# An attention and mixture-of-experts layer on one core: four planned columns of heads, and float16 projections dealt out in half tiles

## The chip, the cores and the metric

The kernel runs on one core of a Trainium2 chip. A core has a matmul engine (TensorE; PE in the profile, with PEld for its weight loads), a vector engine (DVE), a scalar engine (ACT), a general engine (POOL) and a queue engine (SP) that issues most transfers. The metric is the device time of one execution in microseconds (us), the median of several.

## The reference

One transformer layer over 4096 tokens of width 256, in float32. Cut to what matters here:

```
q, k, v = lora(x, Wq, Aq, Bq), lora(x, Wk, ...), lora(x, Wv, ...)   # 16 heads of 16
s   = q @ k.T / 4 + slope[h] * (i - j);  s = -1e30 where j > i       # ALiBi, causal
x   = layernorm(x + (softmax(s) @ v) @ Wp.T)
probs = softmax(x @ Wg);  top 2 of 8 experts, capacity 1076 each
y   = sum over the two of gate * (gelu(x @ W1[e] + b1[e]) @ W2[e] + b2[e])
x   = layernorm(x + y)
```

## The kernel before

**Stages.** First a start-up: effective weights from the low-rank factors, projections of token blocks 0 and 1. Then one long loop over "turns" does attention; projections of blocks 2 to 7 and the routing of blocks 0 to 6 are woven into it. Then the last block is routed, the experts run, and a last layernorm ends.

**A turn.** Tokens come in 8 blocks of 512 queries (QB), keys in tiles of 128. A head needs only `TILES[h]` key tiles, since the bias kills distant ones: 2, 3, 4, 6, 8, 12, 16, 23 and then 32 eight times. Heads 2i and 2i+1 are a pair, which shares its rows of the operand tiles `kop` and `qop` (one at partition 0, one at 64). `plan()` deals pairs to two lanes; a unit is one key tile of one pair, and a turn has one unit of each lane. Its length in a lane is that of the longer head of the pair, and the shorter head leaves its place empty. On the diagonal a key tile needs only the queries from `q0` on, so a unit is 512, 384, 256 or 128 queries wide.

In turn t, PE makes the scores of the turn's two units into `ps_s` (L1024, float16), then `pv(t - LAG)`, LAG being 2: four probability-times-value products in float32 (L1040), one in each group of 32 columns of the array, all into the bank `ps_o`. ACT takes the exponential of each unit (L1097, one instruction for both heads). `ps_s` holds three units (SLOTS_S), so PE may score unit p once the exponential of unit p - 3 is done. POOL zeroes the masked corner of a diagonal unit (L1119). When a job (a pair over all its key tiles) has ended, DVE copies the lane's half of `ps_o` to `acc` (`evict`, L1149), SP stores it, and the first product of the lane's next job waits for the copy.

**Woven in**, all through the one bank `ps_r`, by tables from turn to work: `TILE_AT` (a projection tile, 128 outputs by 512 tokens, two float32 matmuls by `pe_half`, L439, one ahead of `pv` and one behind it, then `dve_head` and `dve_tail`), `VALUE_AT` (values of 128 tokens, L460), `NORM_AT` (norms for an overflow bound, L450), `ROUTE_AT` (output projection and router logits of 128 tokens, L1369) with `SCALE_AT` two turns ahead of it (DVE: shuffle, reciprocal, multiply, L1395 to L1399), `CHOOSE_AT`, `COUNT_AT` and `SCATTER_AT` (top two, places, indirect stores by POOL). Projection tiles stand 3 turns apart, value tiles 2, routing tiles 3. Projections of a block end long ahead of its first turn: the last stand at turn 197, and the loop has 430 turns.

**The flag.** DVE works out whether the float16 scheme is in range (L578 to L589). At `FLAG_TURN`, turn 202, every engine but POOL reads the flag and jumps over the general path (class `General`), which this data does not take. Routing starts behind it.

## Time and profile before

| | |
|---|---|
| median of 3 runs | 1354.06 us (1353.83 to 1354.3) |
| the profiled execution | 1366.05 us |
| its span, first to last instruction | 1363.6 us |
| busy over the span | PE 1208.5, ACT 919.7, DVE 604.4, POOL 352.9 us |
| first exponential of attention | at 41.5 us |
| last one | ends at 873.7 us |

"Busy" of an engine is the union of its instructions. A matmul's end is modelled, so the start-to-start distance says more than its length. Next to each group stands how long its engine was idle just before it and who released it. PEclk is the granted clock of TensorE, 1.00 for 2.4 GHz and 0.50 for 1.2 GHz.

### The profile page before, as it was taken

What the parts mean: (1) busy time and instruction counts of PE and PEld (TensorE: products, weight loads), DVE (VectorE), ACT (ScalarE), POOL (GpSimd) and SP (SyncE); (2) the same over time, 40 slices, a digit from 0 to 9 for tenths busy, and PEclk for the clock granted to TensorE, in tenths of its full rate; (3) what the DMA queues carried; (4) which work ended last, traced back from release to release, by engine and by line L of the source; (5) the groups of instructions that cost most, each with busy time, mean ns of one, the idle gap of its engine ahead of it and who ended that gap; (6) DMA issues with size and microseconds to landing.
All of it is one profiled execution on the core that took longest, in us unless ns stands there. A gap on an engine that the chain in (4) does not pass through costs nothing. (4 is left out here: it accounts for less than half of the span.)

```text
span 1363.6 us, 23733 instructions
## 1 busy us (share of the span) xinstructions
PE 1208.5 (89%) x8566; PEld 500.0 (37%) x8566; DVE 604.4 (44%) x1635; ACT 919.7 (67%) x1200; POOL 352.9 (26%) x374
## 2 busy tenths in 40 slices
PE   7799999999998999999899989625999998999990
PEld 3222222222222212222212211113877876877780
DVE  4232222212122265555446430073676676676756
ACT  2588888888987998899889999514354354344314
POOL 2321211100010013222330330023435534534430
PEclk9899999999999999999998998956999999999995
DMA  6952323213122021402211100154235333322216
GB/s 150 174 104 70 89 84 82 75 62 72 38 67 49 20 63 57 105 31 75 64 58 50 35 33 5 42 175 149 44 103 120 41 100 104 59 72 26 30 20 246
DMA packets 81187, 103.71 MB, mean 76 GB/s; under 512 B 12394, under 2 KB 66389, under 8 KB 81073
## 3 DMA queue, kind: packets, MB, share of 16 engines
q1 hardware_dynamic: 63952, 77.23, 20.7%
q0 software_dynamic: 15744, 23.83, 8.3%
q10 hardware_dynamic: 1376, 1.18, 0.5%
q8 instruction: 65, 1.06, 0.3%
q14 instruction: 50, 0.40, 0.1%
HBM read 56.76 MB, written 48.01 MB: 77 GB/s over the span
## 5 line engine op out<-in xcount | busy, mean ns | idle before, releaser
L1097 ACT ACTIVATE prob<-ps_s 128x1024 f32<-128x1024 f32 (+3 forms) x859 | 721.9, 984 | 118.0 <-PE ps_s L1024 111.8
L1040 PE MATMUL ps_o<-prob,v_aug 128*17 128x512 f32 (+3 forms) x3294 | 443.5, 575 | 17.2 <-DVE acc L1149 6.2
L1024 PE MATMUL ps_s<-qop,kop 51*128 51x512 f16 (+3 forms) x1647 | 280.5, 373 | 33.1 <-ACT prob L1097 10.5
L1024 PEld LDWEIGHTS ps_s<-qop,kop 51*128 51x128 f16 x1647 | 67.5, 93 | 407.0 <-ACT prob L1097 334.8
L1792 PE MATMUL ps_y<-w2s,hs 128*128 128x256 bf16 (+1 forms) x1728 | 199.5, 273 | 0.6 <-DVE yb L1869 0.6
L1776 PE MATMUL ps_h<-xs,w1s 128*128 128x384 bf16 (+1 forms) x1152 | 182.9, 318 | 7.8 <-ACT hid L1839 7.0
L1839 ACT ACTIVATE hid<-ps_h,b 128x384 f32<-128x384 f32 (+1 forms) x192 | 105.1, 560 | 123.0 <-PE ps_h L1776 95.1
L1119 POOL TENSOR_SCALAR_AFFINE_SELECT prob<-prob 128x256 f32<-128x256 f32 (+1 forms) x172 | 67.9, 402 | 436.7 <-ACT prob L1097 434.7
L1792 PEld LDWEIGHTS ps_y<-w2s,hs 128*128 128x128 bf16 (+1 forms) x1728 | 167.4, 99 | 18.2 <-DVE yb L1869 0.7
L1733 POOL DMA_INDIRECT result<-y,entry x72 | 112.0, 1555 | 179.6 <-DVE y L1874 149.2
L1149 DVE COPY acc<-ps_o 64x512 f32<-64x512 f32 x64 | 44.1, 689 | 232.4 <-PE ps_o L1040 223.6
L1776 PEld LDWEIGHTS ps_h<-xs,w1s 128*128 128x128 bf16 x1152 | 111.8, 99 | 73.2 <-ACT hid L1839 10.5
L1040 PEld LDWEIGHTS ps_o<-prob,v_aug 128*17 128x17 f32 x3294 | 58.3, 95 | 162.4 <-issue 105.3
L1885 DVE TENSOR_TENSOR hs<-hid,hs 128x384 bf16<-128x384 f32 (+1 forms) x192 | 105.9, 552 | 6.6
L1883 DVE CAST hs<-hid 128x384 bf16<-128x384 f32 (+1 forms) x192 | 87.9, 458 | 43.3 <-ACT hid L1839 42.4
L1830 ACT ACTIVATE xs<-ps_x 128x512 bf16<-128x512 bf16 (+1 forms) x72 | 40.1, 570 | 93.1 <-PE ps_x L1764 93.1
L1522 POOL DMA_INDIRECT slots_x<-xsplit,dest_all x64 | 63.8, 996 | 106.7 <-DVE xsplit L1500 65.1
L1633 POOL TENSOR_TENSOR w1s<-w,w1s 128x2048 bf16<-128x2048 f32 x8 | 32.5, 4067 | 107.8 <-ACT w1s L1627 92.5
L1869 DVE TENSOR_TENSOR yb<-ps_y,b 128x256 f32<-128x256 f32 (+1 forms) x72 | 30.3, 421 | 60.6 <-PE ps_y L1792 58.4
L1397 DVE RECIPROCAL den<-den 128x256 f32<-128x256 f32 x32 | 56.1, 1753 | 1.1
L439 PE MATMUL ps_r<-x_all 128*128 128x512 f32 x96 | 54.0, 644 | 0.0
L1874 DVE TENSOR_SCALAR y<-yb,weight 128x256 f32<-128x256 f32 (+1 forms) x72 | 45.9, 638 | 13.4 <-DMA result<-y,entry 8.4
(148 smaller groups left out, 651.0 us busy)
## 6 DMA issues: line engine op xcount, KB each, us to landing
w<-in_W SPq DMA_DIRECT2D x16, 1024.0 KB, 7.6
slots_x<-empty POOLq DMA_DIRECT2D x12, 520.0 KB, 4.0
qop<-fparts_q SPq DMA_DIRECT2D x42, 128.0 KB, 4.5
xe<-slots_x SPq DMA_DIRECT2D x8, 650.0 KB
x_all<-in_xT SPq DMA_DIRECT2D x8, 512.0 KB, 5.7
fparts_k<-x_all SPq DMA_DIRECT2D x16, 256.0 KB, 2.2
fparts_q<-x_all SPq DMA_DIRECT2D x16, 256.0 KB, 2.4
attnT<-acc SPq DMA_DIRECT2D x128, 32.0 KB
```

The costliest lines, as they stand in the source:

```text
L1024: mm = pe.matmul(ps_s[:, u.p % SLOTS_S, e, u.q0:], o.key(e, u.i, u.kt), o.query(e, u.i, u.b, u.q0), start=True, stop=True)
L1040: mm = pe.matmul(ps_o[c:c + VW, u.q0:], o.v[:, u.kt, 2 * u.i + e], prob[:, t % RING, n, e, u.q0:], start=u.first, stop=end)
L1097: act.activation(prob[:, t % RING, n, u.heads[0]:2, u.q0:], ps_s[:, u.p % SLOTS_S, u.heads[0]:2, u.q0:], ACT.Exp, scale=1.0 / (SCALE * SCA ...
L1119: pool.affine_select(own, own, [[0, len(u.heads)], [1, P]], ALU.is_ge, 0.0, base=0, channel_multiplier=-1).then_inc(masked, 1)
L1397: dve.reciprocal(r.den[:, s % 2], r.den[:, s % 2]).then_inc(r.inverted, 1)
L1522: pool.indirect_dma_start(out=r.slots_x, out_offset=bass.IndirectOffsetOnAxis(ap=r.dest_all[:, n, m:m + 1], axis=0), in_=r.xsplit[:, m // ...
L1733: pool.indirect_dma_start(out=result, out_offset=bass.IndirectOffsetOnAxis(ap=entry[0:n, u, k:k + 1], axis=0), in_=y[0:n, k % 3], in_offse ...
L1776: mm = pe.matmul(ps_h[:, q % 4, 0:w], w1s[:, u, i1, c, m * P:(m + 1) * P], xs[:, u, i2, c, a:a + w], start=(t == 0 and c == 0), stop=(t == ...
L1792: mm = pe.matmul(ps_y[0:n, (ST * u + k) % 2, 0:D], hs[:, (3 * u + sbk) % 2, i1, m, o:o + n], w2s[:, u, i2, m, :], start=(t == 0 and m == 0 ...
L1839: act.activation(hid[:, q % 4, 0:w], ps_h[:, q % 4, 0:w], ACT.Gelu_apprx_tanh, bias=b1[:, e, q % HC:q % HC + 1]).then_inc(gelu, 1)
L1883: dve.tensor_copy(hs[:, sl, 0, q % HC, 0:w], hid[:, q % 4, 0:w]).then_inc(h_high, 1)
L1885: dve.tensor_tensor(hs[:, sl, 1, q % HC, 0:w], hid[:, q % 4, 0:w], hs[:, sl, 0, q % HC, 0:w], ALU.subtract).then_inc(h_low, 1)
```

## The change

**A plan of four columns.** `columns()` now plans each of the four array columns (two in each lane, one for the heads at partition 0 and one for those at 64) for itself. A column starts its next head as soon as its last has ended, so the two heads of a unit may belong to different pairs and even blocks. Four heads of full length are ordered so that their four diagonal tiles fall in the same turns. Heads 6 and 7 swap their halves of the rows, for which the key and query parts of tiles 0 and 2 are stored with three transfers instead of one, and the bias rows with two more. The loop has 417 turns instead of 430; turns in which the tiles are not all equally wide number 20 instead of 69. Exponentials number 854 (859 before) for the same 780,800 columns; where the two tiles of a unit differ in width, each has its own. Over the turns, the widest tile sums to 199,552 columns (211,328 before). A column that ends is copied alone or with its neighbour: 116 copies (64 before) and 256 stores (192 before).

**Projections in float16 halves.** x and the weights are split into a high and a low float16 part on DVE (`dve_split_x` in four turns for each of six blocks, `dve_split_weights` in four turns once; the last two of each four are maxima for the bound). A half tile is 128 by 256 and takes six float16 matmuls (three part products, two chunks); DVE empties it at once (`dve_half`).

**One piece a turn, spread over 340 turns.** `projections()` spaces the 82 projection pieces evenly up to their due turns; routing pieces take free turns, at least 2 from the next piece. A piece now stands between scores and `pv` of its turn, after a wait that the piece before has left `ps_r`. Routing of block 0 starts at turn 160 (its loads at 150) instead of 214; within a block most routing tiles have a piece 2 turns ahead of them. The set-up of the router stands in turn 76.

**The branch** moves to turn 376, behind the routing, and POOL takes it too. Its general path repeats the routing and is longer. Bias rows of blocks 2 to 7 are loaded with their keys and no longer ahead of the loop. x1 of the routing is kept for two blocks instead of eight.

```
-    for _k in range(4):
-        TILE_AT[_t + 3 * _k] = (_n, _k)
+        due += [(FIRST_TURN[n] - 9, ("half", n, k, h)) for k in range(4) for h in range(2)]
+        due += [(FIRST_TURN[n] - 7, ("norm", n))]
+        due += [(DIAG_TURN[n] - 3, ("value", n, s)) for s in range(KT)]
...
+        z = min(range(i, len(due)), key=lambda z: ((due[z][0] - begin) / (z + 1 - i), -z))
+        for k in range(i, z + 1):
+            at[begin + (due[z][0] - begin) * (k - i) // (z + 1 - i)] = due[k][1]
...
+        for i, (a, b) in enumerate(FPARTS):
+            for c in range(2):
+                mm = pe.matmul(out, j.ws[:, a, m // 2, c, (m % 2) * P:(m % 2 + 1) * P], j.xs[:, b, c, cols],
+                               start=(i == 0 and c == 0), stop=(i == len(FPARTS) - 1 and c == 1))
...
+            dve.tensor_copy(j.xs[:, 0], x).then_inc(j.xs_high, 1)
...
+            dve.tensor_tensor(j.xs[:, 1], x, j.xs[:, 0], ALU.subtract).then_inc(j.xs_done, 1)
...
+                    row = HALF * job.lane + 32 * job.heads[0][0]
+                    rows = slice(row, row + 32 * len(job.heads))
+                    dve.tensor_copy(acc[rows, a], ps_o[rows]).then_inc(evicted[job.lane], 1)
...
-                    if t in TILE_AT:
-                        j.pe_half(pe, *TILE_AT[t], 0, ps_r[:])
+                    if t in PIECE_AT:
+                        bank_free(*BEFORE.get(t, ("norm", 1)))
+                        piece(*PIECE_AT[t])
                     if t >= LAG:
                         pv(t - LAG)
-                    if t in TILE_AT:
-                        j.pe_half(pe, *TILE_AT[t], 1, ps_r[:])
```

On PE, in the projections of block 4, before: `ps_r<-x_all` is half a float32 projection tile, `ps_s` scores, `ps_o` value products.

```order
L1024 MATMUL ps_s<-qop,kop 128x512 x4
L439 MATMUL ps_r<-x_all 128x512
L1040 MATMUL ps_o<-prob,v_aug 17x512 x4
L439 MATMUL ps_r<-x_all 128x512
L1024 MATMUL ps_s<-qop,kop 128x512 x2
L1024 MATMUL ps_s<-qop,kop 128x384 x2
L1040 MATMUL ps_o<-prob,v_aug 17x512 x4
L1024 MATMUL ps_s<-qop,kop 128x384 x2
L1024 MATMUL ps_s<-qop,kop 128x256 x2
L1040 MATMUL ps_o<-prob,v_aug 17x512 x4
```

And after, near the same place: `ps_r<-xs_half,ws_half` is a half tile.

```order
L1234 MATMUL ps_s<-qop,kop 128x512 x4
L1250 MATMUL ps_o<-prob,v_aug 17x512 x4
L1234 MATMUL ps_s<-qop,kop 128x384 x4
L564 MATMUL ps_r<-xs_half,ws_half 128x256 x6
L1250 MATMUL ps_o<-prob,v_aug 17x512 x4
L1234 MATMUL ps_s<-qop,kop 128x256 x4
L1250 MATMUL ps_o<-prob,v_aug 17x512 x4
L1234 MATMUL ps_s<-qop,kop 128x128 x4
L1250 MATMUL ps_o<-prob,v_aug 17x384 x4
```

What moved: a tile's two pieces around one `pv` became one piece ahead of it, and the diagonal widths 384, 256 and 128 stand in all four columns at once instead of in one lane beside a full-width one.

On DVE, in the routing of a block, before: `den` and `aT` are the scale, `slogit` and `x_all` the tile's results, `acc` an eviction of both lanes.

```order
L1397 RECIPROCAL den<-den 128x256
L1399 TENSOR_TENSOR aT<-aT,den 128x2x128
L1403 TENSOR_TENSOR slogit<-ps_r,xg 128x8
L1404 TENSOR_TENSOR x_all<-ps_r,x_all 128x256
L1149 COPY acc<-ps_o 64x512 x2
```

After, in the routing of block 1:

```order
L1641 RECIPROCAL den<-den 128x256
L1643 TENSOR_TENSOR aT<-aT,den 128x2x128
L1390 COPY acc<-ps_o 32x512 x2
L696 TENSOR_SCALAR x_all<-ps_r,less 128x256
L707 SCALAR_TENSOR_TENSOR x_all<-ps_r,less,x_all 128x256
L711 TENSOR_TENSOR sq<-x_all 128x256
L1390 COPY acc<-ps_o 32x512
L1639 STREAM_SHUFFLE den<-total 128x256
```

What moved: between the scales of the routing now stand the halves of block 6 and evictions of single columns.

## Rows read from the trace of the kernel before

**Rows 1.** The page, two groups: count, busy, mean ns, idle before.

```profile
L1097 ACT ACTIVATE prob<-ps_s 128x1024 f32<-128x1024 f32 (+3 forms) x859 | 721.9, 984 | 118.0 <-PE ps_s L1024 111.8
L1040 PE MATMUL ps_o<-prob,v_aug 128*17 128x512 f32 (+3 forms) x3294 | 443.5, 575 | 17.2 <-DVE acc L1149 6.2
```

**Rows 2.** Busy time by stretch: start:end, us, engines (instructions), PEclk, DMA share, GB/s.

```profile
422.00:560.00 138.00, 127.55 (x863) 30.84 (x863) 59.27 (x194) 120.01 (x144) 24.35 (x33) 0.96 0.21 53
...
sum 832.20, PE 785.76 PEld 183.18 DVE 273.18 ACT 721.85 POOL 158.39; mean PE 98.22 PEld 22.90 DVE 34.15 ACT 90.23 POOL 19.80
```

**Rows 3.** Timeline of ACT, two projection tiles: start, us, count, [idle before].

```profile
319.30 5.61 ACT L1097 ACTIVATE prob<-ps_s 128x1024 f32<-128x1024 f32 x6 [1.21 <-PE ps_s L1024]
326.12 5.60 ACT L1097 ACTIVATE prob<-ps_s 128x1024 f32<-128x1024 f32 x6 [1.21 <-PE ps_s L1024]
```

**Rows 4.** Timeline of PE, same stretch: the second half of a tile, then scores.

```profile
317.75 1.13 PE L439 MATMUL ps_r<-x_all 128*128 128x512 f32 x2
...
318.81 0.61 PE L1024 MATMUL ps_s<-qop,kop 51*128 51x512 f16 x4
```

**Rows 5.** Timeline of PE through value tiles two turns apart.

```profile
153.49 1.05 PE L1040 MATMUL ps_o<-prob,v_aug 128*17 128x512 f32 x8 [0.36 <-DVE acc L1149]
...
155.56 0.61 PE L1024 MATMUL ps_s<-qop,kop 51*128 51x512 f16 x4
...
157.08 0.61 PE L1024 MATMUL ps_s<-qop,kop 51*128 51x512 f16 x4
157.62 1.05 PE L1040 MATMUL ps_o<-prob,v_aug 128*17 128x512 f32 x8
158.60 1.16 PE L460 MATMUL ps_r<-x_all 128*128 128x264 f32 x4
159.69 0.61 PE L1024 MATMUL ps_s<-qop,kop 51*128 51x512 f16 x4
```

**Rows 6.** Groups by line in the expert stage, 1250 to 1300 us.

```profile
L1792 PE MATMUL ps_y<-w2s,hs 128*128 128x256 bf16 (+1 forms) x228 | 26.5, 273 | 0.0
...
L1792 PEld LDWEIGHTS ps_y<-w2s,hs 128*128 128x128 bf16 (+1 forms) x229 | 22.1, 99 | 2.4
```

**Rows 7.** Timeline of DVE, PE and ACT in the routing of block 1.

```profile
521.88 1.75 DVE L1397 RECIPROCAL den<-den 128x256 f32<-128x256 f32 x1
...
524.53 0.69 DVE L1149 COPY acc<-ps_o 64x512 f32<-64x512 f32 x1
...
525.37 1.91 PE L1040 MATMUL ps_o<-prob,v_aug 128*17 128x512 f32 x8 [2.04 <-DVE acc L1149]
...
529.53 1.02 ACT L1097 ACTIVATE prob<-ps_s 128x1024 f32<-128x1024 f32 x1 [3.89 <-PE ps_s L1024]
```

**Rows 8.** Timeline at the branch, turn 202, and at the set-up behind it.

```profile
438.31 0.60 PE L1024 MATMUL ps_s<-qop,kop 51*128 51x512 f16 x4 [3.02 <-issue]
...
443.07 1.94 ACT L1097 ACTIVATE prob<-ps_s 128x1024 f32<-128x1024 f32 x2 [2.33 <-PE ps_s L1024]
```

**Rows 9.** Timeline of the start-up: DVE on 512 columns, SP and PE.

```profile
10.28 0.69 DVE L514 SCALAR_TENSOR_TENSOR prob<-prob 128x512 f32<-128x512 f16 x1
11.01 0.43 DVE L516 TENSOR_SCALAR prob<-prob 128x512 f16<-128x512 f32 x1
...
15.01 0.60 SPq L312 DMA_DIRECT2D kop<-bias  x2
...
19.60 1.38 SPq L402 DMA_DIRECT2D fparts_k<-x_all  x2
...
26.05 2.74 ACTq L318 DMA_DIRECT2D qop<-fparts_q  x6
...
40.83 1.36 PE L1024 MATMUL ps_s<-qop,kop 51*128 51x512 f16 x6 [5.58 <-DMA qop<-fparts_q]
```

**Rows 10.** One DVE instruction with two inputs: all eight, then the last.

```profile
L1447 DVE TENSOR_TENSOR gap<-top 128x4 f32<-128x4 f32 x8 | 11.2, 1402 | 0.3
...
910.11 0.17 DVE L1447 TENSOR_TENSOR gap<-top 128x4 f32<-128x4 f32 x1
```

More of the change, by code:

```diff
@@ L88 @@
 assert sorted(TILES) == TILES
[L92 to L108 removed]
+COLS = 4
@@ L120, in plan, with runs @@
         steps.append(step)
     return steps, jobs
-STEPS, JOBS = plan()
+def runs(tiles):
+    if len(tiles) == 2 and tiles[0].q0 == tiles[1].q0:
+        return [(0, 2)]
+    return [(e, e + 1) for e in tiles]
 LAG = 2
@@ L128 @@
 ACCS = 4
+STEPS, JOBS = plan()
+UNITS = [u for s in STEPS for u in s if u]
 N_STEPS = len(STEPS)
-LAST_P = {b: max(u.p for s in STEPS for u in s if u and u.b == b) for b in range(NB)}
+LAST_P = {b: max(u.p for u in UNITS if any(a.b == b for a in u.tiles.values())) for b in range(NB)}
+FREED = {}
+for _n in range(2):
+    for _e in range(2):
+        _ends = [j for j in JOBS if j.lane == _n and any(e == _e for e, _, _ in j.heads)]
+        for _t, _s in enumerate(STEPS):
+            if _s[_n] and _e in _s[_n].tiles and _s[_n].tiles[_e].first:
+                FREED[_t, _n, _e] = max([j.number + 1 for j in _ends if j.end < _t], default=0)
@@ L161 @@
[L161 to L177 removed]
+BLOCK_TURNS = {b: [t for t in range(N_STEPS) for u in STEPS[t] if u and any(a.b == b for a in u.tiles.values())] for b in range(NB)}
@@ L729, in sync @@
                                      y.acc[32 * h + DH:32 * h + VW]).then_inc(y.a_stored, 16)
+            y.attended(sp)
+            for n in range(NB - 1):
+                y.r.load(sp, n, 1)
+                y.r.store_base(sp, n)
             y.leave(sp)
@@ L960, in _ @@
                 j.load_queries(sp, 1)
-                for b in range(2, NB):
-                    o.load_bias(sp, j.bias, b)
                 r.load_constants(sp)
```

634 lines of the change are left out of this document (406 added, 228 removed).

## The prediction

> **What bounds the kernel now.** I read the page first, then the busy time by stretch, then the timelines of single turns. The page gives PE the most busy time, 1208.5 of 1363.6 us, but a matmul's modelled length overlaps its neighbours, so this decides nothing. What the diff touches is the attention loop, 832.2 us, in which ACT is busy for 721.85 [rows 2]: it waits for 110 us, nearly all of it for scores from PE (111.8 of the 118.0 us over the whole kernel) [rows 1]. The exponentials are the same columns before and after (780,800), in 5 instructions fewer. So the loop can't fall under some 722 us, and all that the change can win lies in those 110 us.
>
> Why ACT waits shows in the turns. Six full exponentials take 5.61 us [rows 3] and two take 1.94 [rows 8], so a turn of two costs (5.61 - 1.94) / 2 = 1.83 us. PE needs 1.52 for the same turn: scores start at 155.56 and again at 157.08 [rows 5]. So PE has 0.32 us a turn to spare. What is woven in must fit into it, but for what the three score slots buffer. Rows 3 show a projection tile every third turn: ACT's runs start 6.82 us apart instead of 5.61, 1.21 lost. The sum agrees: a half tile holds PE for 1.06 us (317.75 to 318.81) [rows 4], a tile for 2.1, against 3 x 0.32 = 0.96 to spare; the rest, 1.16, is about the 1.21 idle. A value tile holds PE for 1.09 us (158.60 to 159.69), and with two turns between them the distance is 4.13 us (155.56 to 159.69) [rows 5], 0.46 more than 2 x 1.83. So **the rate of PE's woven-in work over two to four turns** bounds the projection stretches.
>
> Behind 422 us another cause joins: DVE comes late. In rows 7 an eviction starts only at 524.53, since the scale of a routing tile (its reciprocal alone 1.75 us) and its results stood ahead of it. PE then waits 2.04 us, runs on at half clock (products in 1.91 us instead of 1.05), and ACT is idle for 3.89. By stretch PEclk falls to 0.96 there [rows 2]. In the plan of before three evictions stand one turn behind a scale.
>
> **The change part by part**, made against the profiled 1366.05 us (12.0 above the median).
>
> 1. *Projection tiles.* 24 tiles that cost ACT 1.21 us each go: 29.0 us. In their place come 48 halves of six matmuls. A 256-column 16-bit matmul runs at 26.5 / 228 = 0.116 us in the expert stage [rows 6], and a full-array piece costs 0.2 on top (a value tile: 4 x 264 columns at two cycles are 0.88, measured 1.09). So a half is 0.70 + 0.2 = 0.9 us. They stand 2 to 5 turns apart, typically 2.75 in blocks 2 and 3, which gives 0.88 to spare: about nothing is lost. Gain 29, between 22 (0.15 lost at each half) and 31.
>
> The rows show loads of such weights, 229 of 99 ns, beside the matmuls: both in one stretch of 50 us, the 256-column group with its loads covered. The Trainium skill ("TensorE: Matmul & The Clock Gate", Part 3) says that a weight load overlaps a running matmul only when its row group differs, and all rows are used here. The trace does not agree: the 228 matmuls with their loads end to end would need 49 us of PE, and they ran beside 152 others in 50. What uncovered loads would give is rival E.
>
> 2. *Value tiles.* 28 at 0.46 us, 12.9 in all. Their distance to the next piece grows to 2.4 to 4 turns, where 1.09 stands against 0.8 to 1.3. Left over: some 3. Gain 10, between 5 and 13.
>
> 3. *The plan.* ACT's work stays. On PE a product's time follows the widest tile: 11,776 columns fewer at 0.98 us for 512 (157.62 to 158.60 [rows 5]) are 22.5 us. That counts only where PE is late, in the turns around the diagonal next to pieces. I take half, 11; bounds 0 and 22.
>
> 4. *Routing tiles.* Same length and count (28), but from 3 turns apart, which just about fitted (1.09 against 0.96), to 2 behind another piece in most cases. If 17 of them find no slack, 17 x 0.43 = 7 us. Loss 6, bounds 0 and 12.
>
> 5. *Evictions.* 52 more. An eviction at a PE that runs ahead of ACT is free; at a late one it costs the 0.36 us of rows 5 (153.49). Bounds 0 and 19; I take 4, because part 1 gives PE its lead back.
>
> 6. *DVE.* The x and weight splits add 28 instructions on 1024 columns: by rows 9, twice 0.43 for each of 7 high parts and twice 0.69 for the 21 others: 35 us of DVE, which was idle two thirds of the loop. Its cover is the next turn's length; where a split, a scale and an eviction meet (turns 259 to 261) the cover is gone and the cost is a wait as in rows 7. Evictions one turn behind a scale number 4 instead of 3. Loss 5, bounds 0 and 15. POOL shares something with DVE: the same small two-input instruction takes 0.17 us alone and 1.40 on average with POOL at work [rows 10]. The Trainium skill ("SBUF — State Buffer", Who interferes with whom) has a rule for it: a DVE instruction with two inputs or in a two-port mode and one of POOL block each other. The row agrees. Nine of the 28 splits stand in diagonal turns, where POOL's masks gate PE: at 1.38 us each at most 12 us, inside the bound of 15.
>
> 7. *Moved at no cost.* The branch costs the same at turn 376 as at 202 (PE 3.02 us idle, then the set-up, ACT another 2.33 [rows 8]); the flag is long there. POOL takes it when its scatters are issued. The longer bias store (two more transfers and a landing) holds SP from 15.01 on; SP's next store is not ready before 19.60, which leaves 4.6 us. The first score waits for queries that ACT issues at 26.05 and that land near 40.8 [rows 9]; three transfers instead of one for two tiles move neither. Behind the loop, 490 us, nothing changes.
>
> Sum: -29 - 10 - 11 + 6 + 4 + 5 = **-35 us**. Profiled 1331; on the median, 1354.06 - 35 = **1319 us**.
>
> **Rivals.**
>
> *A. PE gets ahead and stays there.* All 22 us of the plan count, routing and evictions cost nothing, DVE 3: -29 - 10 - 22 + 3 = -58, and two of the waits as in rows 7 lose their half clock, another 4: -62, 1292. For it: the sum of widest tiles falls in just the turns where pieces stand. Against: routing tiles at 2 turns have no slack by rows 5.
>
> *B. PE stays the bound.* Every new eviction costs 0.36 (19 us), routing 12, the plan brings nothing, and a half loses 0.15: -22 - 10 + 19 + 12 = -1, 1353. Half-way between this and the forecast: -18, 1336. For it: the stretches up to 422 us run at PE's rate now.
>
> *C. DVE becomes the gate, slower.* 116 evictions and 28 splits share a queue with 28 scales, each a reciprocal of 1.75 us [rows 7] and two more instructions, and the halves' three instructions each, now in the same turns. Each meeting costs what rows 7 show, 3.9 us of ACT with the low clock. It takes (35 + 3) / 3.9 = 10 more meetings than in before to end slower; 14 would give 1374. Against: the plan's table has one more by the strict count, and DVE is busy 273 of 832 us.
>
> *D. It doesn't do what it says.* Waits on `ps_r` or for the split of x take the place of the shorter matmuls, within 2 us of 1354. Against: the high and low parts are made 5 and 4 turns ahead of the first half.
>
> *E. Uncovered weight loads.* Six loads of 0.099 us [rows 6] in each of 48 halves lie on PE: 28.5 us, of which little is covered; -35 + 25 = -10, 1344. Against it are rows 6 themselves, in which they are covered.
>
> **How the numbers follow.** Forecast (1305 to 1333) 0.50; A (under 1305) 0.17; B 0.17, of which 0.15 under 1351; E 0.02; D 0.04, of which 0.03 within 0.2%; C 0.10. The range takes in A's value and B to beyond its half-way: 1290 to 1345, with B's upper part, D and C left out, under 0.2. A measurement here can tell 0.2% (2.7 us) from no change. Faster: 0.50 + 0.17 + 0.15 + 0.02 + 0.01 = 0.85; same 0.02 + 0.03 = 0.05; slower 0.10.
>
> **What would show it.** Right: the loop takes some 797 us from first to last exponential with ACT's busy time still near 722; around a half, PE's next row starts 0.9 us later and ACT shows no idle time; value tiles show gaps under 0.2. Part 4 is right if ACT's remaining gaps stand in 422 to 700 us behind routing tiles. Wrong for part 1: halves of over 1.2 us or gaps of 0.5 behind them. Wrong for parts 5 and 6: waits of PE for evictions of over 25 us in all (6.2 now [rows 1]), or a PEclk under 0.95 in a stretch. Wrong for part 7: a first score after 43 us, or a tail of other than 490 us.

## The result: 0.7% faster, a quarter of what was forecast

The changed kernel takes 1345.12 us (median of 4 runs, 1343.81 to 1346.38), the kernel before on the same chip 1354.18 (1353.83 to 1354.59): ratio 0.9933, 95% interval 0.9916 to 0.995. That is 9 us less; 35 were forecast.

The runs were made in six groups, each on one chip, and the groups fell on two levels: in three of them the kernel before takes 1354 to 1356 us, in three 1364 to 1366. They are called the **1355 level** and the **1365 level** here, and ratios are to the kernel before in the same group. What makes the level isn't known. It doesn't change within a group, but the record has chip number 15 for a group of either level, so it isn't shown to be a property of the chip. The changed kernel gave 0.9933 and 0.9904 at the first level and **1.012** at the second: the same change is 9 to 13 us faster or 14 us slower. The profiled execution of before (1366.05 us) agrees with the second level, the profiled execution of after (1345.55) with the first, so the 20.5 us between the two profiles flatter the change. Single executions at a lower granted clock, 200 to 630 us longer than the others, occurred in a few groups, and the ratios leave them out.

**The page of after**, the groups that answer to rows 1, and the half tiles:

```profile
L1330 ACT ACTIVATE prob<-ps_s 128x1024 f32<-128x1024 f32 (+3 forms) x854 | 721.3, 980 | 101.9 <-PE ps_s L1234 100.5
L1250 PE MATMUL ps_o<-prob,v_aug 128*17 128x512 f32 (+3 forms) x3294 | 422.6, 575 | 29.0 <-DVE acc L1390 18.3
...
L564 PE MATMUL ps_r<-xs_half,ws_half 128*128 128x256 f16 x288 | 40.0, 275 | 9.1 <-DVE x_all L1648 4.3
```

ACT's work is what it was (721.3 us; 721.9 in rows 1), and its idle time fell only from 118.0 to 101.9. What PE waits for evictions rose from 6.2 to 18.3 us. The third line holds a wait of a kind that was nearly absent before: PE waits until DVE has emptied `ps_r`. By the groups of PE in the loop:

```profile
L564 PE MATMUL ps_r<-xs_half,ws_half 128*128 128x256 f16 x288 | 40.0, 275 | 9.1 <-DVE x_all L1648 4.3 <-DVE x_all L709 2.2 <-DVE xg L720 1.3
L580 PE MATMUL ps_r<-x_all 128*128 128x264 f32 x112 | 34.4, 432 | 1.6 <-DVE x_all L1648 1.6
L1613 PE MATMUL ps_r<-wp,aT 128*128 128x264 f32 x112 | 32.7, 415 | 8.6 <-DVE x_all L1648 4.9 <-DVE x_all L707 2.2 <-DVE xg L720 1.5
...
L1618 PE MATMUL ps_r<-counts,before 128*128 128x32 bf16 x7 | 1.3, 186 | 3.2 <-DVE xg L720 1.5 <-DVE x_all L709 0.9 <-DVE run L1708 0.7
```

With two small groups more these waits are 24.3 us (1.7 before). Together with the evictions PE waits 42.6 us for DVE where it waited 7.9, as the profile names its waits.

The names leave out a part. Some waits of the products are put down to ACT or to "issue" (9.1 us before, 8.8 after). But the exponentials of a product are two turns old by then, and each of these waits ends 0.10 or 0.15 us behind the end of an eviction, just as those put down to DVE do. Counted so, PE waits for evictions 15.4 us before and 27.1 after. An example from the version with both repairs (below), DVE and then PE:

```profile
146.24 0.68 DVE L1391 COPY acc<-ps_o 32x512 f32<-32x512 f32 x1
147.02 1.05 PE L1250 MATMUL ps_o<-prob,v_aug 128*17 128x512 f32 x8 [0.31 <-ACT prob L1330]
```

**By stretch**, as rows 2 (start:end, us, then busy time and instructions of PE, PEld, DVE, ACT and POOL, PEclk, DMA share, GB/s):

```profile
422.00:560.00 138.00, 123.38 (x909) 31.94 (x902) 78.68 (x228) 120.39 (x139) 29.57 (x39) 0.99 0.22 60
560.00:700.00 140.00, 127.24 (x916) 31.95 (x916) 69.32 (x231) 120.82 (x138) 28.29 (x36) 0.96 0.22 59
...
sum 815.43, PE 740.77 PEld 185.92 DVE 344.07 ACT 721.36 POOL 158.93; mean PE 123.46 PEld 30.99 DVE 57.35 ACT 120.23 POOL 26.49
```

The loop takes 815.4 us from first to last exponential (832.2 before, at the other level), with PE 45 us less busy and DVE 71 us more (344.07 against 273.18).

**Where the loop loses time.** I take each turn from the end of its last exponential back to that of the turn before, and subtract what its exponentials need back to back (0.917 us for 1,024 columns by rows 3 and 8: (5.61 - 1.94) / 4; 0.702, 0.488, 0.27 and 0.17 for 768, 512, 256 and 128 by the same traces). The excess is put down to the piece that stands in the turn before it:

| excess of ACT's turns, us | before | after | after, both repairs (below) |
|---|---|---|---|
| projection: 24 tiles, then 48 halves | 38.1 | 27.0 | 18.8 |
| 28 value tiles | 22.4 | 19.6 | 18.4 |
| routing tiles and counts | 28.5 | 29.9 | 20.8 |
| norms, set-up | 0.5 | 2.4 | 1.6 |
| turns behind no piece | 36.8 | 31.1 | 22.5 |
| sum | 126.4 | 110.0 | 82.1 |

The column of before is at the 1365 level and the two others at the 1355 level, so a part of the differences is the level's; it is sized below.

By block the changed kernel won 25 us in blocks 2 to 4 (52.5 before, 27.6 after), lost 5 in blocks 0 and 1, and lost 11 in block 6 (17.0, then 28.3).

**One place where it is lost.** PE, DVE and ACT in the projections of block 3, in the order of the engines:

```profile
155.02 0.61 PE L1234 MATMUL ps_s<-qop,kop 51*128 51x512 f16 x4
155.56 1.05 PE L1250 MATMUL ps_o<-prob,v_aug 128*17 128x512 f32 x8
156.55 0.61 PE L1234 MATMUL ps_s<-qop,kop 51*128 51x512 f16 x4
158.35 0.83 PE L564 MATMUL ps_r<-xs_half,ws_half 128*128 128x256 f16 x6 [1.19 <-DVE x_all L709]
```

```profile
156.68 0.70 DVE L1390 COPY acc<-ps_o 32x512 f32<-32x512 f32 x1 [3.12 <-PE ps_o L1250]
157.41 0.42 DVE L698 CAST x_all<-ps_r 128x256 f16<-128x256 f32 x1
157.87 0.42 DVE L709 TENSOR_TENSOR x_all<-ps_r,x_all 128x256 f16<-128x256 f32 x1
```

```profile
155.51 3.77 ACT L1330 ACTIVATE prob<-ps_s 128x1024 f32<-128x1024 f32 x4 [0.22 <-PE ps_s L1234]
160.58 2.85 ACT L1330 ACTIVATE prob<-ps_s 128x1024 f32<-128x1024 f32 x3 [1.29 <-PE ps_s L1234]
```

A half issued at 153.28 was done by 154.04. But DVE's queue holds an eviction ahead of emptying it, and that eviction waits for the products that PE starts at 155.56. So DVE is idle for 3.12 us with a full `ps_r`, empties it at 157.41, and the next half, which stands right behind the scores of its turn, waits 1.19 us and holds the products and the next scores behind it. ACT pays 1.29.

**The worst place**, turn 264, where an eviction of two columns, a maximum, a scale and the half that follows meet. DVE, then PE and ACT:

```profile
555.99 1.41 DVE L1390 COPY acc<-ps_o 32x512 f32<-32x512 f32 x2 [2.44 <-PE ps_o L1250]
557.43 1.22 DVE L681 TENSOR_REDUCE peak<-xs_half 128x1 f32<-128x1024 f16 x1
...
559.05 1.75 DVE L1641 RECIPROCAL den<-den 128x256 f32<-128x256 f32 x1
...
561.37 0.41 DVE L1648 TENSOR_TENSOR x_all<-ps_r,x_all 128x256 f32<-128x256 f32 x1
```

```profile
561.84 1.06 PE L564 MATMUL ps_r<-xs_half,ws_half 128*128 128x256 f16 x6 [2.70 <-DVE x_all L1648]
562.84 1.91 PE L1250 MATMUL ps_o<-prob,v_aug 128*17 128x512 f32 x8
```

```profile
565.39 2.86 ACT L1330 ACTIVATE prob<-ps_s 128x1024 f32<-128x1024 f32 x3 [4.42 <-PE ps_s L1234]
```

PE waits 2.70 us for `ps_r`, its products then run in 1.91 us instead of 1.05 (half clock, as in rows 7), and ACT is idle for 4.42 us. The two evictions in a row of 555.99 are of a kind too: where columns of both lanes end in one turn, the second lane's next product waits for both copies.

### The profile page after: what moved, and what is told of

Read it like the earlier page. It is cut to its first block and busy times, and to the rows that moved or that the text cites. A ratio compares the mean times of both kernels' runs of the same rounds, so it can differ in the third digit from the quotient of the medians.

```text
span 1343.8 us, 24544 instructions
## 1 busy us (share of the span) xinstructions
PE 1164.5 (87%) x8759; PEld 503.3 (37%) x8759; DVE 676.8 (50%) x1791; ACT 918.9 (68%) x1195; POOL 353.4 (26%) x382
## 5 line engine op out<-in xcount | busy, mean ns | idle before, releaser
L1330 ACT ACTIVATE prob<-ps_s 128x1024 f32<-128x1024 f32 (+3 forms) x854 | 721.3, 980 | 101.9 <-PE ps_s L1234 100.5
L1250 PE MATMUL ps_o<-prob,v_aug 128*17 128x512 f32 (+3 forms) x3294 | 422.6, 575 | 29.0 <-DVE acc L1390 18.3
L1234 PE MATMUL ps_s<-qop,kop 51*128 51x512 f16 (+3 forms) x1647 | 267.1, 372 | 26.8 <-ACT prob L1330 8.9
L1390 DVE COPY acc<-ps_o 32x512 f32<-32x512 f32 (+1 forms) x116 | 79.7, 687 | 307.7 <-PE ps_o L1250 300.1
L1234 PEld LDWEIGHTS ps_s<-qop,kop 51*128 51x128 f16 x1647 | 62.4, 94 | 404.9 <-ACT prob L1330 360.1
L2138 DVE CAST hs<-hid 128x384 bf16<-128x384 f32 (+1 forms) x192 | 91.6, 477 | 46.0 <-ACT hid L2094 44.9
L2140 DVE TENSOR_TENSOR hs<-hid,hs 128x384 bf16<-128x384 f32 (+1 forms) x192 | 102.1, 532 | 6.6
L2129 DVE TENSOR_SCALAR y<-yb,weight 128x256 f32<-128x256 f32 (+1 forms) x72 | 48.6, 675 | 12.5 <-DMA result<-y,entry 7.6
L564 PE MATMUL ps_r<-xs_half,ws_half 128*128 128x256 f16 x288 | 40.0, 275 | 9.1 <-DVE x_all L1648 4.3
```

Source lines behind the costliest of these rows:

```text
L1234: mm = pe.matmul(ps_s[:, u.p % SLOTS_S, e, a.q0:], o.key(e, a.h, a.kt), o.query(e, a.h, a.b, a.q0), start=True, stop=True)
L1250: mm = pe.matmul(ps_o[c:c + VW, a.q0:], o.v[:, a.kt, a.h], prob[:, t % RING, n, e, a.q0:], start=a.first, stop=a.last)
L1330: act.activation(prob[:, t % RING, n, e:z, q0:], ps_s[:, u.p % SLOTS_S, e:z, q0:], ACT.Exp, scale=1.0 / (SCALE * SCALE)).then_inc(exp_done, 1)
L1390: dve.tensor_copy(acc[rows, a], ps_o[rows]).then_inc(evicted[job.lane], 1)
L2138: dve.tensor_copy(hs[:, sl, 0, q % HC, 0:w], hid[:, q % 4, 0:w]).then_inc(h_high, 1)
L2140: dve.tensor_tensor(hs[:, sl, 1, q % HC, 0:w], hid[:, q % 4, 0:w], hs[:, sl, 0, q % HC, 0:w], ALU.subtract).then_inc(h_low, 1)
```

## The experiments

All ratios are to the kernel before in the same group of runs, with the 95% interval.

**The kernels themselves, in other groups.** Nothing is edited.

> The changed kernel itself, beside its variants on one chip. In the runs so far the variants showed stalls of ACT and DVE of 2 to 6 us in the turns of the scatters (both wait for updates from PE that come late), 12 to 19 us in all, and the changed kernel, on another chip, none. If these stalls belong to the chip or to the dense scatters in any of the new plans (theory S), they show here too, 10 us or more, and the ratio rises from 0.993 toward 1.000. If they come from what the variants changed (theory V), there are none, and the ratio is again 0.992 to 0.995.

1378.66 us where before has 1364.57: 1.012 (1.0089 to 1.0152). Up to turn 180 its turns exceed ACT's own time just as in the first profile (10.3, 6.9 and 10.4 us in blocks 2 to 4 in both). Then 23.3, 43.0 and 26.7 stand against 17.1, 28.3 and 14.4, and the new losses are at turns 190, 221, 255, 282, 310, 341 and 370 and next to them, one place in each of the seven blocks, in the eight turns in which POOL issues its scatters, as theory S has it.

> The changed kernel once more, as the measure for the three beside it on the same chip. It gave 0.9933 on one chip and 1.012 on another, where ACT waited 2 to 5 us for updates from PE that came late, each time behind five or more scatters that POOL had issued back to back (1.29 us apart). If that depends on the chip: either value, near 0.993 or near 1.01. If it is chance from run to run: something between, with a wide spread.

1342.91 us where before has 1355.7: 0.9904 (0.9886 to 0.9922), none of these losses. So it isn't chance from run to run: it goes with the level. The kernel before was also profiled once more, at the 1365 level: 1363.35 us, its excess some 125 us and spread over the kinds of piece as in the table. It had been expected near 1354 if the first profile held unusual waits, or near 1366 if profiling costs 12 us as such; neither holds, since executions of that group without a profile took 1365.88 too. There is no profile of it at the 1355 level.

**The piece behind the products on PE.**

```
+                    if t >= LAG:
+                        pv(t - LAG)
                     if t in PIECE_AT:
                         bank_free(*BEFORE.get(t, ("norm", 1)))
                         piece(*PIECE_AT[t])
-                    if t >= LAG:
-                        pv(t - LAG)
```

> The changed kernel with the piece back behind the products of its turn on PE (as a value tile stood in before); DVE's order as in the changed kernel. Theory Q: the wait for ps_r comes when DVE has long been released by these products, so waits for ps_r fall below 6 us as well, and the time is 1328 to 1337 us. Theory R: 1341 to 1347 us. If this gains and the other order on DVE doesn't (or the other way round), the cause is where the piece stands and not the wait.

At the 1365 level 1352.72 us, 0.9901 (0.987 to 0.9932), which is 0.022 under the changed kernel in another group of that level. The waits for `ps_r` fell from 24 to 7 us, those for evictions from 18 to 6. But the losses in the scatter turns were there. This edit alone was never run at the 1355 level. The next runs are about the scatters.

**Scatters spaced.** One every second turn, and with a wait for the exponentials of the turn before (two edits in one, never tried apart):

```
-        SCATTER_AT[_t + 2 + _k] = (_n, _k)
+        SCATTER_AT[_t + 2 + 2 * _k] = (_n, _k)
...
+                        pool.wait_ge(exp_done, max(u.exps for u in STEPS[t - 1] if u))
                         r.scatter(pool, *SCATTER_AT[t], r.scattered)
```

> The changed kernel with the scatters of a block in every second turn instead of every turn, each behind the exponentials of the turn before it, so that POOL issues them about 3.7 us apart and no longer in one run of 1.29 us apiece. Theory S (the dense run of scatters makes PE's updates late; the old plan had fewer such runs, since masks stood between its scatters): no wait of ACT over 2.2 us behind scatters, and on a chip like the second 15 to 25 us faster than the changed kernel, ratio 0.990 to 0.996; on a chip like the first within 3 us of it. Rival (the stalls come from the loads and stores that meet there, or from the chip alone): within 5 us of the changed kernel on either chip.

At the 1355 level 1342.71 us, 0.991 (0.9892 to 0.9928): nothing, as expected there of both theories, so it told nothing apart.

> The scatters spaced as in the run before, and the piece issued by PE behind the value products of its turn instead of ahead of them, so that an eviction no longer waits for the piece. Queue theory (42 us of PE's waits for DVE are the order of the two queues): PE's waits for ps_r and evictions fall under 15 us, excess of ACT's turns some 15 us less than with spacing alone, so a ratio of 0.980 to 0.986. Rate theory (what holds ACT up around pieces is PE's own time, whichever comes first): within 4 us of spacing alone.

In the same group **1318.65 us, 0.9723** (0.9706 to 0.9741): 24 us less than with spacing alone. The queue theory's ratio was 0.980 to 0.986; it gave more. Rate theory in its plain form falls, since PE's work is the same to the instruction. Once more in a later group:

> Both edits, scatters spaced and the piece behind the value products, once more, as the measure for the three beside it. It gave 0.9723 on a chip on which the kernel before takes 1355.7 us. On that chip: 0.970 to 0.975 again. If the chip is the slower one (1365 us), the late updates behind scatters should be gone too (theory S): no wait of ACT over 2.2 us in the scatter turns, ratio 0.970 to 0.978; if spacing does nothing there, 0.985 to 0.992, as with the piece behind the products alone (0.9901).

1317.16 us, 0.9721 (0.9704 to 0.9737), again at the 1355 level. Its page and its groups for `ps_r`:

```profile
L1330 ACT ACTIVATE prob<-ps_s 128x1024 f32<-128x1024 f32 (+3 forms) x854 | 719.0, 1000 | 76.2 <-PE ps_s L1234 74.8
```

```profile
L1250 PE MATMUL ps_o<-prob,v_aug 128*17 128x512 f32 (+3 forms) x3294 | 418.8, 571 | 20.9 <-ACT prob L1330 8.8 <-DVE acc L1391 6.2 <-issue 2.5
...
L564 PE MATMUL ps_r<-xs_half,ws_half 128*128 128x256 f16 x288 | 39.8, 274 | 2.1 <-DVE x_all L1649 2.1
L580 PE MATMUL ps_r<-x_all 128*128 128x264 f32 x112 | 34.0, 428 | 0.0
L1614 PE MATMUL ps_r<-wp,aT 128*128 128x264 f32 x112 | 32.3, 411 | 2.3 <-DVE x_all L1649 2.1
```

PE's waits for DVE by name went from 42.6 to 13.1 us (with the misnamed ones, from 51.4 to 24.4), ACT's idle time from 101.9 to 76.2, the loop from 815.4 to 787.5. The same place as above, two halves of block 3 (PE):

```profile
150.29 0.61 PE L1234 MATMUL ps_s<-qop,kop 51*128 51x512 f16 x4
...
151.27 1.05 PE L1250 MATMUL ps_o<-prob,v_aug 128*17 128x512 f32 x8 [0.37 <-ACT prob L1330]
...
152.26 0.83 PE L564 MATMUL ps_r<-xs_half,ws_half 128*128 128x256 f16 x6
153.02 0.61 PE L1234 MATMUL ps_s<-qop,kop 51*128 51x512 f16 x4
```

DVE still does its steps in the same order (eviction at 150.43, emptying at 151.16 and 151.62). But the half now stands behind the products of its turn, one microsecond later in PE's queue, and no longer waits. At turn 264 PE waits 1.47 us instead of 2.70, the clock stays up, and ACT is idle for 1.57 instead of 4.42.

Then the pair that was left, which fell on the 1365 level: the piece behind the products alone, and with the scatters spaced.

> The piece behind the value products, scatters as in the changed kernel. On a chip on which the kernel before takes some 1355 us: within 3 us of the version with spaced scatters, ratio 0.970 to 0.976, since spacing alone did nothing there. On one of some 1365 us: 0.987 to 0.993 as before, with four or more waits of ACT over 2.2 us behind dense scatters.

> The same with the scatters spaced. On a chip of 1355 us: 0.970 to 0.975. On a chip of 1365 us: if dense scatters make the late updates (theory S), 0.970 to 0.980 and no wait of ACT over 2.2 us in the scatter turns; if the late updates are the chip's alone, within 0.003 of the version beside it.

1351.27 us, 0.9909 (0.9888 to 0.993), and **1319.46 us, 0.9666** (0.9647 to 0.9684). Spacing the scatters is worth 32 us there, and the version with both takes the same 1317 to 1319 us at either level. ACT's waits of over 2.2 us in the scatter turns number six in the first and none in the second. The first, with dense scatters (PE, ACT and POOL):

```profile
516.53 0.61 PE L1234 MATMUL ps_s<-qop,kop 51*128 51x512 f16 x4
...
517.02 1.94 ACT L1330 ACTIVATE prob<-ps_s 128x1024 f32<-128x1024 f32 x2 [0.23 <-PE ps_s L1234]
...
518.05 0.60 PE L1234 MATMUL ps_s<-qop,kop 51*128 51x512 f16 x4
...
519.30 0.98 POOL L1777 DMA_INDIRECT slots_x<-xsplit,dest_all  x1 [0.30 <-issue]
...
520.58 0.98 POOL L1777 DMA_INDIRECT slots_x<-xsplit,dest_all  x1 [0.30 <-issue]
521.46 1.94 ACT L1330 ACTIVATE prob<-ps_s 128x1024 f32<-128x1024 f32 x2 [2.50 <-PE ps_s L1234]
...
523.08 1.91 PE L1250 MATMUL ps_o<-prob,v_aug 128*17 128x512 f32 x8
...
525.82 2.90 ACT L1330 ACTIVATE prob<-ps_s 128x1024 f32<-128x1024 f32 x3 [2.42 <-remote]
```

Scores of 516.53 release ACT 0.49 us later; those of 518.05 release it 3.41 us later, behind the fifth and sixth scatter of an unbroken run 1.29 us apart. PE's clock is halved behind the stall (1.91). "remote" is how the profile names an update for which it has no instruction close in time. The second, with spaced scatters:

```profile
524.20 0.98 POOL L1778 DMA_INDIRECT slots_x<-xsplit,dest_all  x1 [2.98 <-ACT prob L1330]
525.60 3.77 ACT L1330 ACTIVATE prob<-ps_s 128x1024 f32<-128x1024 f32 x4 [0.36 <-PE ps_s L1234]
...
528.33 0.98 POOL L1778 DMA_INDIRECT slots_x<-xsplit,dest_all  x1 [3.15 <-ACT prob L1330]
```

**How much the late updates cost.** The traces settle this for every run. Where ACT has waited for scores, its exponential usually starts 0.49 us after the start of the unit's last score matmul. Adding up ACT's waits in which this took more than 0.8 us:

| us of ACT's waiting behind late scores | 1355 level | 1365 level |
|---|---|---|
| before (two profiles) | not profiled | 8.9, 9.2 |
| changed kernel | 0, 0 | 26.8 |
| piece behind the products | not profiled | 28.9, 26.7 |
| scatters spaced, piece ahead | 0 | not profiled |
| both repairs | 0, 0 | 0 |

So the kernel before has these waits too, at turns 268, 297, 344 to 345 and 396 to 397, in its own scatter turns or just behind them. They are about the 10 us by which its two levels differ, and the changed kernel's 26.8 are most of the 34 us by which its levels differ. No run has before with its scatters spaced, so for before this stays a matching of sizes.

**The order on DVE.** The piece of the turn before is emptied ahead of evictions and splits, first in the changed kernel, then with both repairs:

```
-                    for job in STORE_AT[t]:
-                        evict(job)
-                    (splits)
                     if t - 1 in PIECE_AT:
                         ...
+                    for job in STORE_AT[t]:
+                        evict(job)
+                    (splits)
```

> The changed kernel with DVE's order within a turn turned round: the piece of the turn before is emptied out of ps_r first, and evictions and splits come behind it. Theory Q (queue order): DVE holds the emptying back behind an eviction that itself waits for products which PE issues only behind the next piece, so PE waits 24 us for ps_r in the changed kernel. Then these waits fall below 6 us, ACT's idle time from 94 to some 80, and the time to 1328 to 1336 us. Theory R (rate): PE's woven-in work and narrow turns bound it and the waits fall into time that would be lost anyway: 1341 to 1347 us, with the waits gone all the same. If evictions now come late instead, PE's waits for them rise from 18 us to over 30 and nothing is gained.

1369.84 us at the 1365 level, 1.0035 (1.0021 to 1.0049), 9 us under the changed kernel in another group of that level. It won 8 us in blocks 0 to 4, waits for `ps_r` fell to 13 us, and those for evictions rose to 22 by name; the stalls in the scatter turns were there.

> The same with DVE emptying the piece of the turn before ahead of the evictions and splits of the turn. PE still waits 7.0 us for ps_r and 6.2 us for evictions. The products stand ahead of the piece now, so an eviction's product is ready earlier than the next piece: if the order on DVE must follow the order on PE (queue theory), the eviction should go first and this is slower, 2 to 10 us, with more waits for evictions. If what matters is only to free ps_r soon: 3 to 5 us faster, and the best version.

1317.28 us, 0.9727 (0.971 to 0.9743), beside 0.9721 without the edit: no difference. Both of its theories missed. Waits for `ps_r` 5.9 (6.9 without), for evictions by name 8.4 (6.2): one against the other. So it is PE's place for the piece that matters; with that mended, DVE's order doesn't.

**Float32 halves.** Two float32 matmuls in place of six float16 ones, no splits:

```
-        for i, (a, b) in enumerate(FPARTS):
-            for c in range(2):
-                mm = pe.matmul(out, j.ws[:, a, m // 2, c, ...], j.xs[:, b, c, cols], ...)
+        for c in range(2):
+            mm = pe.matmul(out, j.weff[:, m // 2, c, ...], j.xT[:, n % 2, c, cols], ...)
```

> The changed kernel with the 48 half tiles in float32 (two matmuls of 256 columns, as before in kind) straight from the loaded x and weights, and without the 28 splits and maxima on DVE (the range bound leaves out the part on x and weights). PE: a half takes some 1.05 us instead of 0.76, 14 us more in all. DVE: 35 us less. If the float16 form is what the change gains by, the time rises by 8 to 14 us, to 1353 to 1359. If DVE's lateness is what holds the changed kernel back, the splits' going pays for the longer halves: 1340 to 1347 us, with fewer waits for evictions (18 us now).

1394.39 us at the 1365 level, 1.0205 (1.0174 to 1.0235), 12 to 16 us over the changed kernel in another group, with the stalls in both. Cleaner with both repairs:

> The same with float32 halves: two float32 matmuls in place of six float16 ones, no splits of x and of the weights and no maxima (the bound is taken over ones in their place). A half then holds PE for some 1.06 us instead of 0.76, 48 times, 14.4 us more; DVE has 30 us less to do. Rate theory: 10 to 15 us slower than the first of this call. If DVE's splits cost as much as the shorter matmuls save: within 3 us.

1328.03 us, 0.9807 (0.979 to 0.9823): **10.9 us slower** than float16 halves in the same group. Halves lose 0.64 us each on average instead of 0.39. The rate theory's 10 to 15.

**Diagonals of the lanes four turns apart**, in the changed kernel and with both repairs:

```
+            other = [m for m in (meet + KT, meet - KT, meet) if all(0 <= m - begun[c] <= KT * b for c in (2, 3))][0]
             for c, h in enumerate(four):
-                k = meet - begun[c]
+                k = (other if c >= 2 else meet) - begun[c]
```

> Undoes the alignment alone: the diagonal tiles of the second lane's heads come 4 turns later (or earlier) than those of the first; the same exponentials, the same pieces, the same 417 turns. The widest tiles of the turns then sum to 208,768 columns (199,552 with the alignment), 17.6 us of PE more. Rate theory (PE is late for its own work in the turns around the diagonal, the prediction's step 3): 8 to 11 us slower than the changed kernel, ratio about 1.000 to the kernel before. Queue theory (PE is late because it waits for DVE, and a narrow diagonal turn only makes it wait sooner): within 3 us of the changed kernel, and the waits for ps_r fall.

1382.52 us, 1.0128 (1.0092 to 1.0164) beside 1.012, at the 1365 level.

> The same with the diagonals of the two lanes four turns apart: 9,216 columns more in the widest tiles, 17.6 us of PE by 0.98 us for 512. The prediction's step 3 counted half: 9 us slower than the first of this call. On top of the changed kernel itself the same edit cost 1 us (1.0128 beside 1.012, each within 0.35%), which the queue theory explains by PE waiting for DVE anyway; with those waits gone it should now show: 6 to 12 us. Rival (narrow turns starve ACT, so that alignment is worth nothing in itself): within 3 us.

1319.24 us, 0.9739 (0.9718 to 0.9761) beside 0.9721: 2 us, with intervals that overlap. Alignment is worth nothing to some 6 us, not 11, and the rate theory's 6 to 12 is all but out. The plan of four columns as a whole wasn't undone in any run.

**Routing tiles three turns behind their scale.**

```
-        _t = free_turn(_t + 2, ("route", _n, _s))
+        _t = free_turn(_t + 3, ("route", _n, _s))
```

> Routing tiles stand at least 3 turns behind their scale instead of 2, so that a reciprocal, its multiply, evictions and the emptying of a piece are spread over more turns; everything else is as in the changed kernel. The prediction's step 4 (a tile costs 0.43 us where it has no slack): 4 to 7 us faster than the changed kernel. Queue theory: also faster, 5 to 10 us, through fewer waits for evictions in blocks 5 and 6, where the excess of ACT's turns was 17 and 28 us. If neither holds (what costs there is not the distance of routing tiles): within 2 us.

1352.43 us at the 1365 level, 0.992 (0.9898 to 0.9941): 26 us faster than the changed kernel beside it, far more than any theory had. Its excess falls from 43.0 to 22.4 us in block 6. The same edit with both repairs:

> Both edits, and routing tiles three turns behind their scale. If the distance of routing tiles matters by itself (the prediction's step 4: 4 to 6 us), it is that much faster than the run before it. If the gain of the third edit, when it was made alone (20 us beside the changed kernel on the second chip), came from where it put the scatters and not from the tiles, it is within 3 us of the run before it.

With both repairs, 1321.56 us, 0.9753 (0.9735 to 0.977) beside 0.9723: no gain, perhaps 3 us lost. The edit also moves the counts and scatters to other turns. In the run alone ACT's waits behind late scores are 14.1 us instead of 26.8, which is half of the 26 us; the other half is open. Neither run tells of the distance between a routing tile and the piece before it: that stays at 2 turns for 23 of the 28 tiles (25 without the edit).

**No maxima.** Neither of x nor of the weights:

```
-                    if t in SPLIT_W_AT:
+                    if t in SPLIT_W_AT and SPLIT_W_AT[t] < 2:
...
-                    if t in SPLIT_X_AT:
+                    if t in SPLIT_X_AT and SPLIT_X_AT[t][1] < 2:
```

> Leaves out the 14 maxima and minima of the float16 parts (12 of 1.21 us in the loop, 2 in its first turns), which guard the float16 range; the bound is taken over ones in their place. Takes 17 us of DVE away, nothing else. The prediction's step 6 (splits cost 5 us, of 35 us of DVE): 2 to 3 us faster than the changed kernel. Queue theory with DVE's length as the cause: 5 to 8 us faster, waits of PE for ps_r and for evictions down from 42 to under 32 us. If DVE's order and not its length is the cause: within 1 us.

1375.32 us, 1.0084 (1.0048 to 1.0121) beside 1.012 (1.0089 to 1.0152): 3 us by the medians, 5 by the ratios, with intervals that overlap. It can't tell the prediction's 2 to 3 from the queue theory's 5 to 8.

## Why the prediction was wrong, step by step

**The step that failed.** The sum has no term for waits on `ps_r`. Rival D named them (waits on `ps_r` take the place of the shorter matmuls) and got 0.04, with an argument about the splits of x alone. The part on the change mentions the products only as covered by PE's lead and never asks, as it should for a moved step, which queue now stands behind it. The runs show 24.3 us of such waits in the changed kernel and 12 us more for evictions than before, and a gain of 24 us when the piece moves behind the products (1342.71 to 1318.65). The rival that should have been written is the chain of the first example: products, eviction, emptying, next half, products. That both waits and time fall with this edit is shown; through which of the two waits the 24 us come is not.

**The sum as a whole.** With both repairs the same parts give -38 us (0.9721) where -35 was forecast. That nearness is luck, as the parts show. At one level, 1365, where both were profiled, the excess of before and of the version with both repairs is: projection tiles 38.1 and 19.1 us, value tiles 22.4 and 18.9, routing tiles and counts 28.5 and 21.0, turns behind no piece 36.8 and 25.5. So the tiles gave 10 us less than forecast and the value tiles 6 less, and routing, which was to lose 6, gained 8. Some 9 us of before's excess are its late updates, in the last two of these kinds.

**1. Projection tiles** (-29 forecast, -11 by the table, -19 with the repairs). The size of a half is right: by PE's timeline it holds PE from 133.36 to 134.12, 0.76 us, and 0.9 was estimated.

```profile
133.36 0.83 PE L564 MATMUL ps_r<-xs_half,ws_half 128*128 128x256 f16 x6
134.12 0.13 PEld L1250 LDWEIGHTS ps_o<-prob,v_aug 128*17 128x17 f32 x8 [0.21 <-ACT prob L1330]
```

The next instruction starts when six matmuls of 0.127 us each are done; the loads (0.098 us each in a group of 288) are beside them. Rival E is out. The Trainium skill ("TensorE: Matmul & The Clock Gate", Part 3) says in its list that a load overlaps matmuls only when the row group differs, which isn't borne out here either; the same part also lets a load into the background weight buffer be pulled ahead, and that fits the trace.

"About nothing is lost" was right in one place and wrong in another. With both repairs (the trace of 0.9721), 29 of the 48 halves have only full-width turns beside them. Of these the 23 that stand three turns or more behind the piece before cost 0.1 us on average and mostly nothing: spare time does add up over the turns between. A tile of 1.09 us costs 0.46 in such a turn at a distance of two (11 routing tiles, with no eviction near), as the prediction reckons (1.09 - 2 x 0.32 = 0.45), and still 0.29 or 0.30 at greater distances, again with no eviction near. A float32 half of 1.06 us costs 0.27 by the median at three turns or more. So the spare time grows to 0.6 us over two turns as forecast and then stops near 0.8, where the forecast let it grow on; that three score slots hold no more is the likely reason, not a shown one.

The 19 halves with a narrow diagonal turn at or beside them cost 12.7 of the 18.9 us. A half in a turn of width 128, whose exponentials are short, costs 1.35 us (four of them), a float32 half there 1.65 and a tile of 1.09 us 1.68: these differ by just what the pieces differ in length, so there every further microsecond shows in full. The prediction priced every place like a full-width turn. In the rows, with both repairs, first PE and then ACT: the half of 216.41 stands in a turn of width 128 and ACT waits 1.25 us behind it; those of 221.88 and 229.21 stand in full-width turns and ACT runs through.

```profile
215.42 0.29 PE L1234 MATMUL ps_s<-qop,kop 51*128 51x128 f16 x4
...
216.41 0.83 PE L564 MATMUL ps_r<-xs_half,ws_half 128*128 128x256 f16 x6
...
221.88 0.83 PE L564 MATMUL ps_r<-xs_half,ws_half 128*128 128x256 f16 x6
...
229.21 0.83 PE L564 MATMUL ps_r<-xs_half,ws_half 128*128 128x256 f16 x6
```

```profile
217.66 20.27 ACT L1330 ACTIVATE prob<-ps_s 128x1024 f32<-128x1024 f32 x22 [1.25 <-PE ps_s L1234]
```

The price of the old tiles was off as well: 1.21 us was read at one place, and the 24 tiles cost 1.59 on average.

**2. Value tiles** (-10 forecast, -3, and -4 with the repairs). They cost 0.80 each before, not 0.46, and 0.66 with the repairs, not 0.1. Twelve of the 28 stand at or beside a narrow turn (0.85 each), 13 next to an eviction (0.57), and only three in the plain place that the prediction priced (0.29 or 0.30).

**3. The plan** (-11 forecast). Undoing its alignment costs 2 us, at most some 6. The 22 us of columns are real PE time, but most lie in narrow turns; why they bring so little is open. Turns behind no piece did improve by 6 (14 with the repairs), of which up to 9 are before's late updates.

**4. Routing tiles** (+6 forecast, +1 by the table, -8 with the repairs at one level). At two turns a plain one costs 0.46, as forecast; but before, at three turns, half of the plain ones cost 0.29 or more and not nothing, so the loss is 0.17 each. The gain behind it comes from other places; evictions and late updates stand next to routing tiles in before.

**5. Evictions** (+4 forecast, bounds 0 and 19). PE's waits for them grew by 12 us, by name as counted in full, inside the bounds. With the piece moved they are at 6.2 by name, as before the change, and at 17.5 in full (15.4 before): the 52 more cost 2 us of PE's waiting there.

**6. DVE** (+5 forecast, bounds 0 and 15). The size of the work was right: 71 us more, of which 36 are evictions, 30 splits and maxima, 13 the halves' own steps, and 8 less in the small two-input instructions. Thirteen splits stand in diagonal turns by the plan, and not nine. Its effect in time was its place ahead of emptying `ps_r`; what its length costs is not settled (no maxima: 3 to 5 us, within the noise).

**7. At no cost.** The first exponential is at 41.24 us (41.5 before); over all profiles of changed versions it is at 40.6 to 43.2, so a microsecond or two here is scatter. Behind the loop it takes 487.1 us (490), and 484.7 to 488.0 in all of them (488.6 and 490.0 before): some 3 us less, in a part that the change wasn't to touch. Why is open. The branch costs PE and ACT what it did in rows 8:

```profile
786.06 0.60 PE L1234 MATMUL ps_s<-qop,kop 51*128 51x512 f16 x4 [3.06 <-issue]
786.55 3.77 ACT L1330 ACTIVATE prob<-ps_s 128x1024 f32<-128x1024 f32 x4 [2.23 <-PE ps_s L1234]
```

**What was in no step.** (a) The change moved the scatters without a term of their own for it, and at the 1365 level their place costs 27 us (9 before). Of the 49 distances between scatters within a block, 26 are under 1.4 us before and 47 in the changed kernel: in the old plan masks of diagonal tiles stood on POOL between many of them; the new one leaves POOL free turns, and it runs them off 1.29 us apart. (b) The sum was made against a profile 12.0 us above the median, and the difference subtracted as if it touched nothing. That profile was of the 1365 level. Without its late updates before's excess would be some 118 us, an estimate from the traces of that level (126.4 - 8.9), since before was never profiled at the 1355 level. The changed kernel's 110.0 is 8 less, near the 9 us of the result.

**Still open:** why the updates of PE's scores come late during an unbroken run of indirect scatters, and what makes the level of a group. The share of the DMA engines at those moments was anything from 0.13 to 1.2, so a full DMA load isn't the sign of it.

## What to carry to other kernels

When a step is moved in one engine's queue, write out the ring through the other engine's queue: what it waits for, which instruction stands ahead of that release, and whether that one waits for something now queued behind the moved step. A shared buffer that is emptied behind an unrelated wait acts like a missing buffer; giving the refill the latest place in its turn was worth 24 us of 1343 here. Spare time on a feeding engine adds up only to a limit (here 0.8 us, reached in three turns), and where the fed engine's work is short a woven-in piece shows in full, so price each kind of place by itself, with rows of such a place, and not one place for all. Don't take the name beside a wait for its cause when the engine named had long been done. And take the profile that a sum is made against from a run that agrees with the median it is to forecast.

## What the runs showed of the hardware

- The same program differs by 0.8% between groups of runs (before: 1354 to 1356 us, or 1364 to 1366), and the changed kernel by 2.6% (1343 to 1345, or 1379). The version with both repairs takes 1317 to 1319 us at either level.
- At the slower level, scores' completions reached ACT up to 3 us late (3.41 us instead of 0.49 after the start of the matmuls) while POOL issued indirect scatters back to back; one every second turn took the effect away, 32 us. With spaced scatters, or at the faster level, no such delay went beyond 0.8 us in nine profiles.
- A full-height 128x128 float16 weight load costs nothing to be seen beside 256-column matmuls of other weights: six in 0.76 us, with loads of 0.098 us each.
- A product that waits for an eviction starts 0.10 or 0.15 us behind the eviction's end, whatever releaser the profile names (15.4 us of such waits before and 27.1 after, of which 6.2 and 18.3 are put down to DVE by name).
